# A decoder in one launch: its recurrence with another layout, a wider bias product, squares on ACT, and drains of POOL's queue inside three phases

## The reference

```
r = decay * r + kt * vt                  # kt and vt are both the context of step t
inp = (qt * r) @ Wi.T + bi               # qt is x of step t
gate = sigmoid(inp @ Wg.T + bg)
blended = gate * state + (1 - gate) * inp
state = tanh(blended @ A.T + inp @ Bm.T)
out = state @ Wo.T + bo                  # then x6 = layernorm(x5 + out)
```

## Time and profile before

| | us |
|---|---|
| median of 3 runs | 1576.53 |
| lowest, highest | 1567.0, 1576.57 |
| the profiled execution's own time | 1574.4 |
| its span, first to last instruction | 1572.6 |

### The profile page before, as it was taken

The page is one execution under the profiler, slowest core; times in us unless marked ns, Lnnn a source line. Parts: engine busy times, 40 slices in busy tenths (PEclk is TensorE's granted clock), DMA queues, the critical chain, the costliest instruction groups (busy, mean ns, idle before and its releaser), DMA issues. The chain is left out here.

```text
span 1572.6 us, 32540 instructions
## 1 busy us (share of the span) xinstructions
PE 1270.7 (81%) x9948; PEld 844.5 (54%) x9949; DVE 1117.2 (71%) x3370; ACT 787.8 (50%) x2133; POOL 561.0 (36%) x828
## 2 busy tenths in 40 slices
PE   4799999999999998708888599999986999819920
PEld 2456666666666655404554255555554887607710
DVE  3578888878888887537887599999984444437744
ACT  2678878787877875301221166666662323312200
POOL 1233335344444434340000655656413234530045
PEclk9999999999999998659999599999995556759965
DMA  7000000000000000002221700000000000111123
GB/s 265 15 14 18 15 18 25 20 23 23 22 23 22 15 13 19 19 29 59 63 64 54 279 22 23 24 23 24 10 1 2 13 24 24 33 40 56 55 82 89
DMA packets 83241, 65.53 MB, mean 42 GB/s; under 512 B 11809, under 2 KB 77986, under 8 KB 82210
## 3 DMA queue, kind: packets, MB, share of 16 engines
q1 hardware_dynamic: 71410, 46.06, 9.3%
q0 software_dynamic: 6656, 13.64, 2.8%
q10 hardware_dynamic: 5040, 4.11, 0.8%
HBM read 40.70 MB, written 23.07 MB: 41 GB/s over the span
## 5 line engine op out<-in xcount | busy, mean ns | idle before, releaser
L608 PE MATMUL e_bank_turned<-c_matrices,e_probs 128*128 128x128 f32 x1024 | 165.8, 286 | 16.2 <-ACT e_probs_t L840 9.0
L840 ACT ACTIVATE e_probs_t<-e_bank_turned 128x512 f32<-128x512 f32 x256 | 155.0, 605 | 15.7 <-PE e_bank_turned L608 14.4
L545 POOL TENSOR_TENSOR e_rstd<-e_var_eps,c_minus_half 128x1 f32<-128x1 f32 x128 | 71.3, 571 | 251.7 <-DVE e_var_eps L876 251.3
L962 DVE TENSOR_REDUCE e_neg_max<-e_bank_scores 128x4 f32<-128x512 f32 x160 | 109.5, 684 | 51.1 <-PE e_bank_scores L651 50.7
L608 PEld LDWEIGHTS e_bank_turned<-c_matrices,e_probs 128*128 128x128 f32 x1024 | 116.4, 145 | 39.9 <-issue 15.4
L1246 PE MATMUL m_wide<-up,m_rowsT 128*128 x224 | 119.6, 616 | 9.1 <-issue 8.2
L618 PE MATMUL e_bank_mix<-e_probs_t,e_values 128*32 128x128 f32 x2048 | 113.2, 294 | 15.6 <-ACT e_probs_t L840 15.2
L799 ACT ACTIVATE e_probs<-e_scores,e_neg_max 128x128 f32<-128x128 f32 x384 | 123.2, 409 | 1.1 <-DVE e_neg_max L998 1.1
L1695 ACT ACTIVATE d_probs_t<-d_bank_turned 128x512 f32<-128x512 f32 x128 | 76.6, 598 | 65.9 <-PE d_bank_turned L1580 65.7
L1303 DVE TENSOR_TENSOR m_pre<-m_wide,up_b 128x512 f32<-128x512 f32 x112 | 77.4, 691 | 36.6 <-PE m_wide L1246 36.1
L548 POOL TENSOR_TENSOR e_k_by_place<-e_q_k_k,c_matrices 128x512 f32<-128x512 f32 x64 | 66.6, 1041 | 102.8 <-DVE e_q_k_k L1006 102.8
(11 more groups left out here) (311 smaller groups left out, 3310.6 us busy)
## 6 DMA issues: line engine op xcount, KB each, us to landing
m_rows<-scratch_sorted SPq DMA_DIRECT2D x112, 64.0 KB, 1.8
scratch_expert_out<-m_y SPq DMA_DIRECT2D x112, 64.0 KB, 1.6
e_x_in<-in_x SPq DMA_DIRECT2D x32, 64.0 KB, 1.9
e_ctx_in<-in_ctx SPq DMA_DIRECT2D x32, 64.0 KB, 2.1
up<-in_m_wgv SPq DMA_DIRECT2D x1, 2048.0 KB, 8.2
up_b<-in_m_bgv SPq DMA_DIRECT2D x1, 2048.0 KB, 14.6
scratch_ctxT<-e_xT_ctxT SPq DMA_DIRECT2D x32, 64.0 KB, 1.5
scratch_x<-e_x SPq DMA_DIRECT2D x32, 64.0 KB, 1.7
```

Source lines behind the costliest of these rows:

```text
L608: last = nc.tensor.transpose(turned_bank[:, j * P:(j + 1) * P], pr[k % 3][:, j, :], c["ident"][:])
L840: nc.scalar.activation(pt[k % 2][:], turned_bank[:], ACT.Copy).then_inc(probs_t_ready, 1)
L962: nc.vector.tensor_reduce(nmax[k % 4][:], bank, AX.X, ALU.max, negate=True).then_inc(max_ready, 1)
```

## The change

The states and xT_all lie as [feature, step, sequence]: the 32 values of one step are side by side. The rows of a tile are therefore step first, sequence second, and the last store turns them back. The bias product takes all 128 rows: `first_row` is a [128, 128] tile whose first row is ones and the rest zeros, and bo is loaded into all partitions. POOL squares only the first two spans; ACT squares the other fourteen, one every eight steps, at offset -23. Part of DVE's setup moves behind the first n_held. POOL's queue gets a `drain()` after each pool_scattered of encode (8), after every fourth gather slot of decode (8), and after every eighth tile of the recurrence (4).

```diff
@@ phase_encode, POOL
                 if (n := group_at(tick, 94)) is not None:
                     pool_scattered(pool, r, n // SLOTS)
+                    pool.drain()
@@
-TICKS_RECUR = range(-17, P + 48)
+TICKS_RECUR = range(-23, P + 48)
@@ recur_buffers, load_recur
-                bo=sb("bo", [1, P]), ...
+                bo=sb("bo", [P, P]), ...
-    sp.dma_start(e["bo"][:], d["n_bo"].rearrange("(o p) -> o p", o=1)).then_inc(e["loaded"], 16)
+    sp.dma_start(e["bo"][:], d["n_bo"].partition_broadcast(P)).then_inc(e["loaded"], 16)
@@ phase_decode, POOL and ACT
+                if (b := due(tick, -28)) is not None and b % 4 == 3:
+                    pool.drain()
-                    nc.scalar.activation(xT_all[:, :, b, :], act_bank[:, 0:P].rearrange("p (n t) -> p n t", t=LINE), ACT.Copy)...
+                    nc.scalar.activation(xT_all[:, :, b], act_bank[:, 0:P], ACT.Copy)...
@@ phase_recurrent
-        states = sb("states", [P, TILES, BATCH, LINE])
+        states = sb("states", [P, P, BATCH])
         def state(t):
-            return states[:, t // LINE, :, t % LINE]
+            return states[:, t, :]
@@ POOL
-            for k in range(SPANS):
+            for k in range(2):
                 part = e["ctxT"][:, :, k * STEPS:(k + 1) * STEPS]
                 nc.gpsimd.tensor_tensor(squares[:, k, :]..., part, part, ALU.mult)\
-                    .then_inc(squared, 1)
+                    .then_inc(first_squared, 1)
...
                 if n >= 8:
                     scatter(n - 8)
+                if n % 8 == 7:
+                    pool.drain()
@@ PE
-                    nc.tensor.matmul(sub[n % 2][:, 0:P], lhsT=ones_row[:], rhs=e["bo"][:], start=False, stop=False)
+                    nc.tensor.matmul(sub[n % 2][:, 0:P], lhsT=first_row[:], rhs=e["bo"][:], start=False, stop=False)
@@ ACT
+                if (k := span_at(tick, -23)) is not None and k >= 2:
+                    nc.scalar.activation(squares[:, k, :].rearrange("p (b t) -> p b t", t=STEPS),
+                                         e["ctxT"][:, :, k * STEPS:(k + 1) * STEPS], ACT.Square).then_inc(squared, 1)
@@ DVE, ahead of the ticks
-            nc.vector.memset(fade[:], 0.0)
-            nc.vector.memset(hot[:], 0.0)
-            nc.vector.memset(ones_row[:], 1.0)
-            nc.vector.tensor_scalar_add(below[:], c["iota8"][:], -float(EXPERTS))
-            last = chain.mark(nc.vector.tensor_copy(kept["taken"][:], c["row_base"][:]))
-            chain.wait(last)
+            chain.wait(chain.mark(nc.vector.memset(fade[:], 0.0)))
             dve.wait_ge(e["loaded"], RECUR_LOADS)
...
-            nc.vector.tensor_scalar_mul(minus_wa[:], e["wa"][:], -1.0).then_inc(set_up, 1)
-            dve.wait_ge(set_up, 1)
@@ DVE, in the ticks
-                    nc.vector.tensor_tensor(held[k % 2][:].rearrange("p (n t b) -> p n t b", t=LINE, b=BATCH), ...
+                    nc.vector.tensor_tensor(by_step(held[k % 2]), by_batch(mem[k % 2]).rearrange("p b t -> p t b"),
+                                            xT_all[:, k * STEPS:(k + 1) * STEPS, :], ALU.mult)\
+                if tick == -14:
+                    nc.vector.tensor_scalar_mul(minus_wa[:], e["wa"][:], -1.0)
+                    nc.vector.memset(hot[:], 0.0)
+                    chain.wait(chain.mark(nc.vector.memset(first_row[:], 0.0)))
+                    nc.vector.memset(first_row[0:1, :], 1.0)
+                    nc.vector.tensor_scalar_add(below[:], c["iota8"][:], -float(EXPERTS))
+                    nc.vector.tensor_copy(kept["taken"][:], c["row_base"][:]).then_inc(set_up, 1)
+                    dve.wait_ge(set_up, 1)
@@ phase_finish, ACT's queue
-                        act.dma_start(out[:, bass.ds(n * LINE, LINE), :], x7[h][s][:])...
+                        act.dma_start(out[:, bass.ds(n * LINE, LINE), :].rearrange("b t d -> t b d"), x7[h][s][:])...
```

More of the change, by code:

```diff
@@ L1438, in recur_buffers @@
     return dict(ctxT=sb("ctxT", [P, BATCH, P]), loaded=nc.alloc_semaphore("recur_loaded"),
-                bo=sb("bo", [1, P]), **{n: sb(n, [P, P]) for n in ("wi", "wg", "wa", "wb", "wo")},
+                bo=sb("bo", [P, P]), **{n: sb(n, [P, P]) for n in ("wi", "wg", "wa", "wb", "wo")},
                 **{n: sb(n, [P, 1]) for n in ("bi", "bg", "decay")})
@@ L1691, in _ @@
                     act.wait_ge(x5_turned, b + 1)
-                    nc.scalar.activation(xT_all[:, :, b, :], act_bank[:, 0:P].rearrange("p (n t) -> p n t", t=LINE), ACT.Copy).then_inc(x5T_ready, 1)
+                    nc.scalar.activation(xT_all[:, :, b], act_bank[:, 0:P], ACT.Copy).then_inc(x5T_ready, 1)
                 if 1 <= tick <= UNITS_ALL:
@@ L1839, in phase_recurrent @@
                              "drive_done"))
+        first_squared = sem("first_squared")
         gated_ready, summed, state_ready = sem("gated_ready"), sem("summed"), sem("state_ready")
@@ L1922, in _ @@
                         pe.wait_ge(x6_ready, n - 1)
-                    nc.tensor.matmul(sub[n % 2][:, 0:P], lhsT=xT_all[:, n, :, :].rearrange("p b t -> p (b t)"), rhs=c["ident"][:],
+                    nc.tensor.matmul(sub[n % 2][:, 0:P], lhsT=xT_all[:, n * LINE:(n + 1) * LINE, :].rearrange("p t b -> p (t b)"), rhs=c["ident"][:],
                                      start=True, stop=False)
-                    nc.tensor.matmul(sub[n % 2][:, 0:P], lhsT=ones_row[:], rhs=e["bo"][:], start=False, stop=False)
+                    nc.tensor.matmul(sub[n % 2][:, 0:P], lhsT=first_row[:], rhs=e["bo"][:], start=False, stop=False)
                 if (n := line_at(tick, 5)) is not None:
                     pe.wait_ge(state_ready, (n + 1) * LINE)
-                    nc.tensor.matmul(sub[n % 2][:, 0:P], lhsT=states[:, n, :, :].rearrange("p b t -> p (b t)"), rhs=e["wo"][:],
+                    nc.tensor.matmul(sub[n % 2][:, 0:P], lhsT=states[:, n * LINE:(n + 1) * LINE, :].rearrange("p t b -> p (t b)"), rhs=e["wo"][:],
                                      start=False, stop=True).then_inc(sub_done, 1)
@@ L2020, in _ @@
             chain = Chain(dve, links, 0, 0)
[L2021 to L2026 removed]
+            chain.wait(chain.mark(nc.vector.memset(fade[:], 0.0)))
             dve.wait_ge(e["loaded"], RECUR_LOADS)
[L2028 to L2031 removed]
+            faded = chain.mark(nc.vector.tensor_copy(fade[:].rearrange("p (b t) -> p b t", t=STEPS)[:, :, 1:STEPS],
+                                                     e["decay"][:].unsqueeze(2).to_broadcast([P, BATCH // 2, STEPS - 1])))
             for tick in TICKS_RECUR:
@@ L2047, in _ @@
                 if (k := span_at(tick, -17)) is not None:
-                    dve.wait_ge(squared, k + 1)
+                    if k < 2:
+                        dve.wait_ge(first_squared, k + 1)
+                    else:
+                        dve.wait_ge(squared, k - 1)
                     if k:
@@ L2056, in _ @@
                         cut = slice(part * SPAN // 2, (part + 1) * SPAN // 2)
-                        if k and part == 0:
+                        if part == 0:
                             chain.wait(faded)
@@ L2155, in _ @@
                         act.wait_ge(x7_ready, LEAD + n + 1)
-                        act.dma_start(out[:, bass.ds(n * LINE, LINE), :], x7[h][s][:]).then_inc(x7_saved[h][s], 16)
+                        act.dma_start(out[:, bass.ds(n * LINE, LINE), :].rearrange("b t d -> t b d"), x7[h][s][:]).then_inc(x7_saved[h][s], 16)
             for h in range(2):
@@ L2284, in program @@
         with ExitStack() as second:
-            xT_all = second.enter_context(nc.sbuf_tensor("xT_all", [P, TILES, BATCH, LINE], F32))
+            xT_all = second.enter_context(nc.sbuf_tensor("xT_all", [P, P, BATCH], F32))
             recur = recur_buffers(nc, second)
```

6 lines of the change are left out of this document (1 added, 5 removed).

## The result

The changed kernel takes 1521.80 us (median of 4 runs, 1518.06 to 1524.99) against 1574.37 (1567.0 to 1576.57): a ratio of 0.9673 (95% interval 0.9632 to 0.9714). The profiled execution took 1522.29 us, its span is 1520.5. Of all kernels here only a_no_bias, further down, had executions in a slower state (1556.49 and 1557.86 us), and its figures are those of its two others.

The account below looks back on a forecast made before the run. The recurrence was taken as bound by a chain of ACT, DVE and PE, with PE fully busy at clock 0.50. Terms -9.8 - 1.5 - 3 - 23 = -37.3 us from 1574.4 gave 1537.1, as median 1539; range 1527 to 1566.

Parts of the forecast that it names:

- The bias product: Recurrence, PE: using 128 rows instead of one costs no PE time, 445 ns against 450 for its neighbour.
- The clock term: Recurrence: full-row bias products lift PE's granted clock from 0.50 to 1.00, 55 steps x 0.42 = -23 us, bound -33.
- lapses of the clock: Recurrence: another 10 to 15 steps are lost when the risen clock falls back for a while.
- The layout: Recurrence: n_gated reads states side by side, 0.03 us less a step; -3 us, between 0 and 3.9 saved.
- The drains: POOL's DRAIN split into pieces in encode, decode and recurrence shortens the phase ends; -9.8 us in sum.
- Encode: End of encode: POOL's final DRAIN of 5.29 us replaced by a last piece of 0.7; -4.6 us.
- Decode: End of decode: 0.17 us of POOL's DRAIN left, earlier pieces fit in its 99.2 us of waiting; -3.9 us.
- the tail: End of recurrence: final DRAIN shrinks from 2.67 to 0.7, the piece adds 0.7; -1.3 us, bounds -1.3 to -0.1.
- The start: Start of recurrence: POOL stops after two squares and DVE's scan starts earlier; -1.5 us, bounds -0.8 to -2.2.
- Squares: Recurrence: fourteen squares moved to ACT fall into its idle time of 0.74 us and cost nothing.
- that rival: Recurrence, ACT: each of 14 squares brings two table loads, 36 us more, giving 1598 us; chance 0.05.
- The last store: Finish: same 64 KB in the other order, 0 in the sum; the skill's rule would add about 1 us.

Follow-up runs that it names:

- a_no_bias: The changed kernel with the bias product left out altogether, so the recurrence's output lacks the bias: 1536.12 us from two executions, ratio 0.976.
- a_64_rows: The changed kernel with 64 of the 128 rows in the bias product: 1544.26 us, ratio 0.9780.
- b_zero_product: The kernel before, one-row bias product kept, with a product of 128 x 128 zeros against the identity added in each tile: 1593.26 us, ratio 1.0117.
- a_no_decode_drains: The changed kernel without the eight drains in decode: 1521.50 us, ratio 0.9661.
- a_no_drains: The changed kernel without any of the twenty drains: 1528.80 us, ratio 0.9708.
- a_pool_squares: The changed kernel with all sixteen squares on POOL again and none on ACT, all drains in place: 1519.74 us, ratio 0.9656.
- b_full_row: The kernel before with the bias product alone made over all 128 rows: 1535.57 us, ratio 0.9732.
- c_drains: The changed kernel with only decode's last drain kept there and none behind the recurrence's last tile: 1517.69 us, ratio 0.9622.
- a_one_row: The changed kernel with its bias product put back to one row: 1567.57 us, ratio 0.9935.
- c_fill: The c_drains kernel with useless full-row products on PE ahead of the first tile, at early ticks and in the last 17 ticks: 1511.23 us, ratio 0.9578.

## Why the prediction was wrong

**The step that failed** is "The bias product. Time on PE: none. 445 ns with one row, 450 for its neighbour with 128". The durations are right and say nothing: PE's ends are modelled, and what counts is when the next product starts. The seam costs 0.4 to 0.6 us a tile at 0.50 and 0.1 at 1.00. At the clocks of before, 24 tiles lay at 0.50 and 8 at 1.00: 24 x 0.6 + 8 x 0.1 = 15 us, or 10 at 0.4 a tile, that the sum had at nothing. With it the forecast would have been 1524 to 1529 and the foot of the range 1512 to 1517, and the measured 1521.80 would have lain inside.

**The clock term held.** That the clock follows the rows is shown apart from the seam by a_64_rows: 35 more steps at 1.00 and 23 us. In the change there are 76 more steps at 1.00. By the eight steps of a kernel with 128 rows (11.8 - 1.2 = 10.6 at 0.50, 7.9 at 1.00) that is 76 x 2.7/8 = 26 us, against my 23; with the seam at 0.4 a tile it is 76 x 3.1/8 = 29. I had 55 steps at 0.42; there were more, and each gained less, since the seam's part isn't the clock's. That it is a matter of rows alone was too simple: see b_zero_product. The 10 to 15 steps that I gave up to lapses of the clock weren't lost: none came, here or in a_no_decode_drains, a_no_drains and a_pool_squares, which have 105 steps at 1.00 each.

**The layout was mis-sized**, at 3 us where 108 x 0.05 = 5.4 came by estimate (b_full_row, which lacks it, has 132.8 us of steps against 126.4, with five fewer at 1.00). I priced what reads the states (n_gated, 0.022 us) and not what writes them (tanh, 0.030). And I had it pay while PE is behind, or not, without asking at which clock: it pays at 1.00, where the chain of tanh, product and matmul sets the pace.

15 + 26 + 5.4 = 46, or 10 + 29 + 5.4 = 45, against the 43.1 measured. So the sum is firm and its split between seam and clock is not. The lighter first and last steps are in none of these prices.

**The drains** were 7 us and not 9.8. Encode gained more than forecast: it takes 672.2 to 675.3 us in the five profiles without drains there and 666.9 to 669.3 in the nine with them. What is above 4.6 isn't accounted for; the low stretches of the clock in encode differ as well. Decode gained nothing that a run shows: I had read POOL's 99.2 us of waiting as slack for a piece, but the first pieces stop POOL for up to 6.4 us before the pipeline is full, and the table load ahead of the phase's first softmax starts 5 us later than before, counted from the barrier (26.7 against 21.7 us; 22.6 in a_no_decode_drains). On the tail the piece cost 2.1 us of gap against 2.67 - 0.70 = 1.97 saved: my upper bound of -0.1, which allowed for a wait for the scatter in flight, and not the -1.3 that I took. The price of 0.083 us for each DMA held where nothing was in flight: 0.700 us for the last eight scatters, and 1.353 for the 16 of c_drains.

**The start** gave 2.7 us, outside my bound of 2.2, but 0.9 of it is luck. The profiled execution had the clock at 1.00 for 3.4 us there, which no part of the change aims at. In the six profiles with the same start at 0.50 (among them a_one_row and a_no_drains) the first state comes 10.7 to 10.8 us after the barrier, 1.7 sooner than before and near my 1.5. **Squares**: no table load came with the fourteen (407 ns each, idle before 0.0), so that rival is refuted. **The last store**: finish is 65.8 to 65.9 us in the three kernels with the old order and 66.2 to 66.6 in the others. The rule of the Trainium skill, "DMA: Bandwidth & Descriptors", section "Why a DMA increments its semaphore by 16 and not by 1", on the slowest dimension asked for about 1 us by my estimate; 0.3 to 0.8 was there, so the traces agree in direction. How many DMA engines shared the store, no view here shows.

## What to carry to other kernels

Read the starts of weight loads beside the products: idle time in front of PEld put down to "issue" was a stall here, although PE is shown busy and the mean duration is normal. A product of few rows between products of 128 wasn't cheap here because it does little; try it with all the rows. In a stage that sits near the edge of the clock, price a change to PE twice, by its time and by what it does to the work per time, and price the parts that set the other engines' pace at the clock that the change will leave.

## What had not been expected

The 127 added rows of `first_row` are zeros, and they moved the clock all the same. Leaving a product out made the changed kernel 14 us slower (a_no_bias, 1536.12 against 1521.80), and 26 useless ones gave 0.4% more than the same kernel without them had gained (c_fill, 1511.23, against c_drains, 1517.69, measured at different times), while 32 useless ones in the wrong place made the kernel before 1.2% slower (b_zero_product). A DRAIN on POOL's queue took 0.70 us after eight finished indirect DMAs, 3.2 behind a scatter and 4.8 to 9.4 behind gathers.
